# Six recurrent layers on one core: another warm-up for TensorE, the first loads in two blocks each, one subtraction moved on GpSimd, and the two waits of a gather exchanged

## The chip, the core and the metric

The kernel runs on one core of one Trainium2 chip. TensorE (PE) multiplies and transposes into PSUM, VectorE (DVE), ScalarE (ACT) and GpSimd (POOL) do elementwise work, and DMA transfers are issued from the queues of SyncE (SP), ACT and POOL. Each engine runs its own list of instructions in order and meets the others through semaphores. The metric is the device time of one execution in microseconds (us).

## The reference

```python
for i in range(6):                       # n_layers
    gate = ih[i][token]                  # ih: 6 x 4000 x 256, token: 1024
    state = jnp.tanh(state + jnp.matmul(state, hh[i]) * gate)   # state: 1024 x 256, hh: 6 x 256 x 256
return state
```

Everything is float32.

## The kernel before, in words

**Layout.** The state is held transposed: 256 features in two blocks of 128 partitions (c = 0, 1), 1024 tokens along the free dimension. A token's six gate rows lie side by side in DRAM, so one indirect DMA (a gather, L249) brings all six layers' gates for 128 tokens. There are eight gathers, t = 0 to 7, issued one after the other by POOL.

**Tokens equal to the last row of the table** are not fetched. That row is loaded once (L297), spread over all partitions by 12 transposes on PE (L588, three pieces of four), and copied into the gate buffers before the gathers 2 to 7 land over it: DVE does the pieces of layers 0 and 1 (L396), ACT the other two pieces (L302). Gather t waits for the copies to its own tile (the function `gather`, L243 to L253). For tiles 0 and 1 the row is patched in afterwards (L404).

**Layer 0** goes in quarters of 256 tokens (q = 0 to 3). For each, PE multiplies in plain float32 (`plain`, L493, eight products of 128 by 256), DVE multiplies by the gates (`gating`, L420), PE turns the result (`turn`, L502), DVE adds the old state (`sum_up`, L425), and ACT takes the tanh twice: rounded to fp32r into `sh` (L310) and in full into `s` (L314). The low part `sl = s - sh` is a subtraction on POOL (L259), for quarter 0 on DVE (L429).

**Layers 1 to 5** are wide: four units per layer, u = (h, c), half h of the tokens (512) by block c of the features. The weights are split in the same way, a high part on ACT (`round_weights`, L306) and a low part on POOL (`low_weights`, L270). A unit's product is three pairs of products of 128 by 512: high by high (L552), low of weights (L559), low of state (L569). The last pair needs the `sl` of its half of the tokens. DVE multiplies by the turned gates (L436) and adds the state (L441), ACT takes two tanhs (L328, L329), POOL makes `sl` (L265). The gates are turned by PE (`turn_gates`, L521) and copied from PSUM by ACT (L322).

**The order around the change** is written out by hand. PE before layer 0: 5 transposes of the identity matrix as a warm-up (L583), which wait for POOL's identity matrix, then the 12 spread transposes, which wait for the last row, then `plain(0)`, `plain(1)`, `turn(0)`, `plain(2)`, `turn_gates(1, 0, 0)`, `turn(1)`. The weights of layer 2 are loaded from SP once gather 5 has landed. ACT rounds them ahead of the tanh of quarter 2, and POOL takes `low_state(1)`, `low_state(2)`, `low_weights(2)`, `low_state(3)` after the last gather. The first use of `sl` of quarters 2 and 3 is `low_product(1, 1, 0)` on PE.

Of the kernel before, what the change touches and what calls it, by code (L numbers as in the profile page):

```python
# [4 lines left out]
P = 128  # L5
# [16 lines left out]
WIDE = 1  # L22
STEPS = WIDE * QUARTERS
UNITS = HALVES * KC
WARM_UP = 5

# [29 lines left out]
def recurrent_cells(nc, state_t, token, gate_rows, hh, out_t):  # L58
# [10 lines left out]
    with ExitStack() as ctx:  # L69
# [3 lines left out]
        def sem(name):  # L73
            return ctx.enter_context(nc.semaphore(name))
# [44 lines left out]
        spread_ready = sem("spread_ready")  # L119
        state_in = quarter_sems("state_in")  # L120
        w_in = [sem(f"w_in{l}") for l in range(LAYERS)]
        gate_in = [sem(f"gate_in{t}") for t in range(TILES)]
        ident_zero = sem("ident_zero")
        ident_ready = sem("ident_ready")
# [42 lines left out]
        def of_quarter(x, q):  # L167
            return x[:, :, q * QB:(q + 1) * QB]
# [22 lines left out]
        with nc.Block() as block:  # L191

            @block.sync
            def _(sp):
                def load_state(q):
                    sp.dma_start(of_quarter(s, q), state_v[q]).then_inc(state_in[q], 16)

                def load_weights(l):
                    sp.dma_start(w[:, l], w_v[l]).then_inc(w_in[l], 16)

                sp.dma_start(tok[:, :], token).then_inc(tok_in, 16)

                sp.wait_ge(ident_ready, 1)
                load_weights(0)
                sp.wait_ge(tok_in, 16)
                load_state(1)
                sp.wait_ge(state_in[1], 16)
                load_state(2)
                sp.wait_ge(gate_in[1], 16)
                load_state(3)  # L210
                sp.wait_ge(gate_in[2], 16)
                load_weights(1)

                for l, t in LOAD_BEHIND.items():
                    sp.wait_ge(gate_in[t], 16)
                    load_weights(l)
                for l in range(4, LAYERS):
                    sp.wait_ge(w_in[l - 2], 16)
                    load_weights(l)

                def store(u, columns):
                    h, c = divmod(u, KC)
                    sp.dma_start(out_v[h, c, :, columns], of_unit(s, h, c)[:, columns]).then_inc(out_done, 16)

                for u in [0, 1]:
                    sp.wait_ge(unit_s[u], wide_done(LAYERS - 1))
                    store(u, slice(0, HB))
                sp.wait_ge(unit_s[UNITS - 2], wide_done(LAYERS - 1))
                store(UNITS - 2, slice(0, QB))
                sp.wait_ge(unit_s[UNITS - 1], wide_done(LAYERS - 1))  # L230
                store(UNITS - 1, slice(0, QB))
                sp.wait_ge(late_s, 1)
                store(UNITS - 2, slice(QB, HB))

                sp.wait_ge(out_done, 16 * (UNITS + 2))

            @block.gpsimd
            def _(pool):
# [5 lines left out]

                def gather(t):
                    if t not in EARLY_TILES:
                        pool.wait_ge(filled_dve, fills_of(t, DVE_FILLS))
                        pool.wait_ge(filled_act, fills_of(t, ACT_FILLS))
                    nc.gpsimd.indirect_dma_start(  # L249
                        gate[:, t], None, table,  # L250
                        bass.IndirectOffsetOnAxis(row_of[:, t:t + 1].bitcast(u32), 0),
                        bounds_check=last_fetched, oob_is_err=False,
                    ).then_inc(gate_in[t], 16)  # L253
# [20 lines left out]
                    gather(t)  # L274
                low_weights(1)
                low_state(1)
                low_state(2)
                low_weights(2)
                low_state(3)
                for l in range(WIDE, LAYERS - 1):  # L280
                    for h in range(HALVES):
# [13 lines left out]
            @block.scalar  # L295
            def _(act):
                act.dma_start(last_row[:, :, :], last_row_v).then_inc(row_in, 16)  # L297
                act.dma_start(of_quarter(s, 0), state_v[0]).then_inc(state_in[0], 16)

                def fill(i, t, count):  # L300
                    act.wait_ge(spread_ready, i + 1)
# [35 lines left out]
                round_weights(1)  # L337
                tanh(1)
                copy_gates(1, 0, 1)
                round_weights(2)  # L340
                tanh_rounded(2)
                tanh(2)
                copy_gates(1, 1, 0)
                tanh_rounded(3)
# [138 lines left out]
            def _(pe):  # L483
                def plain(n):
                    l, q = divmod(n, QUARTERS)
                    pe.wait_ge(w_in[l], 16)
                    if l == 0:
                        pe.wait_ge(state_in[q], 16)
                    else:
                        pe.wait_ge(s_ready[q], l)  # L490
                    for t in range(TPQ):
                        for c in range(KC):
                            last = nc.tensor.matmul(prod[q][:, t, :], of_quarter(s, q)[:, c, t * P:(t + 1) * P], w[:, l, c, :],  # L493
                                                    start=c == 0, stop=c == KC - 1)
                    last.then_inc(prod_ready[q], 1)
# [78 lines left out]
                def end_product(i, ready):  # L574
# [3 lines left out]
                    low_of_weights(l, h, c, end_bank[i], tokens)  # L578
                    low_of_state(l, h, c, end_bank[i], tokens, ready)

                pe.wait_ge(ident_ready, 1)
                for _ in range(WARM_UP):
                    nc.tensor.transpose(turned[0][:, 0, 0:P], ident[:, :], ident[:, :])  # L583
                pe.wait_ge(row_in, 16)
                for i in range(PIECES):
                    columns = spread[i].rearrange("p (m c) -> p c m", m=P)
# [84 lines left out]
```

## Time and profile before

| | us |
|---|---|
| median of three runs | 59.0 |
| the runs | 58.88, 59.0, 60.3 |
| the profiled execution's own time | 59.24 |
| its span, first to last instruction | 57.4 |
| mean granted TensorE clock | 1.000 |

All times of the rows are microseconds from the span's start. The profiled execution's time is 1.84 us more than its span; that part lies around the instructions and is in no row. "Busy" of an engine is the sum of its instructions; the ends of products are modelled, so two neighbours can overlap in the rows by a few tenths.

### The profile page before, as it was taken

The numbers are of one execution on the slowest core, as the hardware profiler recorded it, in microseconds if no ns is written. First come the engines' busy times: TensorE is split into PE (matmuls) and PEld (weight loads), VectorE is DVE, ScalarE is ACT, GpSimd is POOL, SyncE is SP. The second block draws the span as 40 slices with busy tenths as digits, with TensorE's granted clock in tenths as the row PEclk, the third lists the DMA queues.
The fourth block names the chain that finished last, engine by engine and source line by source line (L and its number), as shares of the span: only waits on it lengthen the run. The fifth ranks groups of instructions, "written<-read, shape, count | busy, mean of one in ns | idle before, by whom it ended". The sixth has DMA issues, their size and how long they took to land.

```text
span 57.4 us, 864 instructions
## 1 busy us (share of the span) xinstructions
PE 50.7 (88%) x271; PEld 42.4 (74%) x271; DVE 39.9 (70%) x62; ACT 43.8 (76%) x80; POOL 41.7 (73%) x40
## 2 busy tenths in 40 slices
PE   0899999989999999699999999999999999999000
PEld 0796888949898796488888988679888798889000
DVE  1249996985995498099985949899089990768700
ACT  0714999565944999968998599999999899943810
POOL 2067176777496299992999995899998998659600
PEclk9999999999999999999999999999999999999999
DMA  0479356574463924000000000000000000004392
GB/s 0 14 242 319 89 181 170 165 220 109 71 198 40 318 49 169 0 0 0 0 0 0 0 0 6 0 6 0 0 0 0 11 0 0 0 0 183 126 323 100
DMA packets 5284, 4.46 MB, mean 78 GB/s; under 512 B 1834, under 2 KB 4906, under 8 KB 5280
## 3 DMA queue, kind: packets, MB, share of 16 engines
q1 hardware_dynamic: 3312, 3.28, 18.0%
q0 software_dynamic: 1152, 0.73, 5.5%
q10 hardware_dynamic: 816, 0.40, 3.0%
q8 instruction: 2, 0.03, 0.2%
q14 instruction: 2, 0.02, 0.1%
HBM read 8.92 MB, written 1.05 MB: 174 GB/s over the span
## 4 chain that ended last, share of the span: by engine, by line
PE 47%; DMA 14%; issue 12%; POOL 11%; ACT 5%; DVE 2%; POOLq 1%; SPq 1%
PE prod L569 14%; PE prod L552 11%; PE prod L559 11%; PE turned L521 11%; DMA gate<-gates_dram,row_of 6%; DMA w<-hh_dram 6%; POOL sl L259 4%; DMA tok<-token_dram 3%; POOL pre L289 2%; POOL wr L270 2%; POOL gate L249 2%; POOLq L191 1%; DVE gp L470 1%; ACT wr L306 1%; ACT sh L310 1%
## 5 line engine op out<-in xcount | busy, mean ns | idle before, releaser
L265 POOL TENSOR_TENSOR sl<-s,sh 128x512 fp32r<-128x512 f32 x16 | 20.4, 1299 | 2.6 <-ACT s L329 2.5
L436 DVE TENSOR_TENSOR prod<-prod,gate_t 128x512 f32<-128x512 f32 x17 | 11.8, 697 | 6.9 <-PE prod L569 6.9
L569 PE MATMUL prod<-sl,wr 128*128 128x512 f32 (+1 forms) x42 | 12.5, 387 | 0.5 <-POOL sl L259 0.5
L552 PE MATMUL prod<-sh,wr 128*128 128x512 f32 (+1 forms) x42 | 12.9, 393 | 0.0
L329 ACT ACTIVATE s<-pre 128x512 f32<-128x512 f32 x18 | 11.3, 630 | 1.7 <-POOL pre L289 1.4
L559 PE MATMUL prod<-sh,wr 128*128 128x512 f32 (+1 forms) x42 | 12.4, 381 | 0.0
L441 DVE TENSOR_TENSOR pre<-prod,s 128x512 f32<-128x512 f32 x17 | 11.8, 692 | 0.6
L249 POOL DMA_INDIRECT gate<-gates_dram,row_of x8 | 8.1, 1007 | 5.1 <-DVE row_of L390 1.8
L328 ACT ACTIVATE sh<-pre 128x512 fp32r<-128x512 f32 x16 | 10.3, 641 | 1.9 <-DVE pre L441 1.9
L322 ACT COPY gate_t<-turned 128x512 f32<-128x512 f32 x20 | 10.8, 585 | 0.0
L521 PEld LDWEIGHTS turned<-ident,gate 128*128 128x128 f32 x80 | 9.1, 140 | 1.5 <-issue 0.8
L521 PE MATMUL turned<-ident,gate 128*128 128x128 f32 x80 | 10.1, 273 | 0.0
L569 PEld LDWEIGHTS prod<-sl,wr 128*128 128x128 f32 x42 | 7.6, 188 | 2.7 <-issue 0.9
L559 PEld LDWEIGHTS prod<-sh,wr 128*128 128x128 f32 x42 | 7.8, 188 | 1.6
L552 PEld LDWEIGHTS prod<-sh,wr 128*128 128x128 f32 x42 | 7.4, 189 | 1.1
L493 PE MATMUL prod<-w,s 128*128 128x256 f32 x32 | 8.0, 400 | 0.1
L270 POOL TENSOR_TENSOR wr<-w,wr 128x512 fp32r<-128x512 f32 x5 | 6.5, 1297 | 1.2 <-issue 0.9
L302 ACT COPY gate<-turned 128x512 f32<-128x512 f32 (+1 forms) x8 | 5.8, 829 | 2.0 <-PE turned L588 1.7
L493 PEld LDWEIGHTS prod<-w,s 128*128 128x128 f32 x32 | 6.2, 203 | 1.3 <-DMA w<-hh_dram 0.5
L259 POOL TENSOR_TENSOR sl<-s,sh 128x512 fp32r<-128x512 f32 x3 | 3.9, 1294 | 1.6 <-ACT s L314 1.6
L404 DVE COPY_PREDICATED gate<-is_last,turned 128x512 f32<-128x512 int32 (+1 forms) x4 | 4.0, 1024 | 0.5 <-ACT gate L302 0.5
L306 ACT CAST wr<-w 128x512 fp32r<-128x512 f32 x5 | 3.2, 632 | 1.5 <-DMA w<-hh_dram 1.5
(35 smaller groups left out, 36.8 us busy)
## 6 DMA issues: line engine op xcount, KB each, us to landing
w<-hh_dram SPq DMA_DIRECT2D x6, 256.0 KB, 2.8
s<-state_t_dram SPq DMA_DIRECT2D x3, 256.0 KB
out_t_dram<-s SPq DMA_DIRECT2D x2, 256.0 KB, 2.1
out_t_dram<-s SPq DMA_DIRECT2D x3, 128.0 KB, 2.0
s<-state_t_dram ACTq DMA_DIRECT2D x1, 256.0 KB, 3.5
gate<-gates_dram,row_of POOLq DMA_INDIRECT x8, 3.3
out_t_dram<-s ACTq DMA_DIRECT2D x1, 128.0 KB, 2.3
tok<-token_dram SPq DMA_DIRECT2D x1, 4.0 KB, 1.7
```

The source lines that it names most:

```text
L249: nc.gpsimd.indirect_dma_start(gate[:, t], None, table, bass.IndirectOffsetOnAxis(row_of[:, t:t + 1].bitcast(u32), 0), bounds_check=last_f ...
L265: nc.gpsimd.tensor_tensor(of_unit(sl[:, l % 2], h, c), of_unit(s, h, c), of_unit(sh[:, l % 2], h, c).bitcast(f32), ALU.subtract).then_inc( ...
L322: nc.scalar.copy(gate_t[:, l % 2, u], turned_bank[u][:, :]).then_inc(gates_copied[u], 1)
L328: nc.scalar.activation(of_unit(sh[:, l % 2], h, c), of_unit(pre, h, c), ACT.Tanh).then_inc(unit_sh[u], 1)
L329: nc.scalar.activation(of_unit(s, h, c), of_unit(pre, h, c), ACT.Tanh).then_inc(unit_s[u], 1)
L436: nc.vector.tensor_tensor(prod_bank[u][:, :], prod_bank[u][:, :], gate_t[:, l % 2, u], ALU.mult).then_inc(unit_gated[u], 1)
L441: nc.vector.tensor_tensor(of_unit(pre, h, c), prod_bank[u][:, :], of_unit(s, h, c), ALU.add).then_inc(unit_pre[u], 1)
L493: last = nc.tensor.matmul(prod[q][:, t, :], of_quarter(s, q)[:, c, t * P:(t + 1) * P], w[:, l, c, :], start=c == 0, stop=c == KC - 1)
L521: last = nc.tensor.transpose(turned_bank[u][:, t * P:(t + 1) * P], gate[:, h * TPH + t, column:column + P], ident[:, :])
L552: nc.tensor.matmul(bank, wr[:, l, k, 0, c * P:(c + 1) * P], of_unit(sh[:, (l - 1) % 2], h, k)[:, tokens], start=k == 0, stop=False, skip_g ...
L559: nc.tensor.matmul(bank, wr[:, l, k, 1, c * P:(c + 1) * P], of_unit(sh[:, (l - 1) % 2], h, k)[:, tokens], start=False, stop=False, skip_gr ...
L569: last = nc.tensor.matmul(bank, wr[:, l, k, 0, c * P:(c + 1) * P], of_unit(sl[:, (l - 1) % 2], h, k)[:, tokens], start=False, stop=k == KC ...
```

## The change

Four edits. PE's warm-up is four products of a constant of ones instead of five transposes of the identity matrix; it waits for no semaphore, and the wait for the identity matrix stands behind it. The state of quarter 0 and the weights of layer 0 are each loaded by two DMAs, one per block c, with a semaphore each; `plain(0)` waits for a block ahead of its first product that reads it. POOL's two waits of a gather are exchanged, with the one on ACT's copies now written first. `low_weights(2)` on POOL goes ahead of `low_state(2)`, and on ACT the rounded tanh of quarter 2 goes ahead of `round_weights(2)`.

```diff
--- before.py
+++ after.py
@@ -22,7 +22,7 @@
 WIDE = 1
 STEPS = WIDE * QUARTERS
 UNITS = HALVES * KC
-WARM_UP = 5
+WARM_UP = 4
 
 
 
@@ -119,6 +119,9 @@
         spread_ready = sem("spread_ready")
         state_in = quarter_sems("state_in")
         w_in = [sem(f"w_in{l}") for l in range(LAYERS)]
+
+        first_state_in = [sem(f"first_state_in{c}") for c in range(KC)]
+        first_w_in = [sem(f"first_w_in{c}") for c in range(KC)]
         gate_in = [sem(f"gate_in{t}") for t in range(TILES)]
         ident_zero = sem("ident_zero")
         ident_ready = sem("ident_ready")
@@ -200,8 +203,10 @@
 
                 sp.dma_start(tok[:, :], token).then_inc(tok_in, 16)
 
+
                 sp.wait_ge(ident_ready, 1)
-                load_weights(0)
+                for c in range(KC):
+                    sp.dma_start(w[:, 0, c], w_v[0][:, c]).then_inc(first_w_in[c], 16)
                 sp.wait_ge(tok_in, 16)
                 load_state(1)
                 sp.wait_ge(state_in[1], 16)
@@ -244,8 +249,8 @@
 
                 def gather(t):
                     if t not in EARLY_TILES:
+                        pool.wait_ge(filled_act, fills_of(t, ACT_FILLS))
                         pool.wait_ge(filled_dve, fills_of(t, DVE_FILLS))
-                        pool.wait_ge(filled_act, fills_of(t, ACT_FILLS))
                     nc.gpsimd.indirect_dma_start(
                         gate[:, t], None, table,
                         bass.IndirectOffsetOnAxis(row_of[:, t:t + 1].bitcast(u32), 0),
@@ -274,8 +279,8 @@
                     gather(t)
                 low_weights(1)
                 low_state(1)
+                low_weights(2)
                 low_state(2)
-                low_weights(2)
                 low_state(3)
                 for l in range(WIDE, LAYERS - 1):
                     for h in range(HALVES):
@@ -295,7 +300,8 @@
             @block.scalar
             def _(act):
                 act.dma_start(last_row[:, :, :], last_row_v).then_inc(row_in, 16)
-                act.dma_start(of_quarter(s, 0), state_v[0]).then_inc(state_in[0], 16)
+                for c in range(KC):
+                    act.dma_start(of_quarter(s, 0)[:, c], state_v[0][:, c]).then_inc(first_state_in[c], 16)
 
                 def fill(i, t, count):
                     act.wait_ge(spread_ready, i + 1)
@@ -337,8 +343,8 @@
                 round_weights(1)
                 tanh(1)
                 copy_gates(1, 0, 1)
+                tanh_rounded(2)
                 round_weights(2)
-                tanh_rounded(2)
                 tanh(2)
                 copy_gates(1, 1, 0)
                 tanh_rounded(3)
@@ -483,13 +489,16 @@
             def _(pe):
                 def plain(n):
                     l, q = divmod(n, QUARTERS)
-                    pe.wait_ge(w_in[l], 16)
-                    if l == 0:
+                    if l > 0:
+                        pe.wait_ge(w_in[l], 16)
+                        pe.wait_ge(s_ready[q], l)
+                    elif q > 0:
                         pe.wait_ge(state_in[q], 16)
-                    else:
-                        pe.wait_ge(s_ready[q], l)
                     for t in range(TPQ):
                         for c in range(KC):
+                            if n == 0 and t == 0:
+                                pe.wait_ge(first_state_in[c], 16)
+                                pe.wait_ge(first_w_in[c], 16)
                             last = nc.tensor.matmul(prod[q][:, t, :], of_quarter(s, q)[:, c, t * P:(t + 1) * P], w[:, l, c, :],
                                                     start=c == 0, stop=c == KC - 1)
                     last.then_inc(prod_ready[q], 1)
@@ -578,9 +587,10 @@
                     low_of_weights(l, h, c, end_bank[i], tokens)
                     low_of_state(l, h, c, end_bank[i], tokens, ready)
 
+                ones = nc.const_aps.tensor(1.0, [P, P], f32)
+                for _ in range(WARM_UP):
+                    nc.tensor.matmul(turned[0][:, 0, 0:P], ones, ones, start=True, stop=True)
                 pe.wait_ge(ident_ready, 1)
-                for _ in range(WARM_UP):
-                    nc.tensor.transpose(turned[0][:, 0, 0:P], ident[:, :], ident[:, :])
                 pe.wait_ge(row_in, 16)
                 for i in range(PIECES):
                     columns = spread[i].rearrange("p (m c) -> p c m", m=P)
```

The list of POOL from its first gather to the first wide low state. L249 and L254 are the gathers, L270 and L275 the low weights of layers 1 and 2, L259 and L264 the low states of quarters 1, 2 and 3. Before:

```order
L249 DMA gate<-gates_dram,row_of 128x1536
L249 DMA gate<-gates_dram,row_of 128x1536 [waits filled_act,filled_dve] x6
L270 TENSOR_TENSOR wr<-w,wr 128x2x256 [waits wh_ready]
L259 TENSOR_TENSOR sl<-s,sh 128x2x256 [waits s_ready1]
L259 TENSOR_TENSOR sl<-s,sh 128x2x256 [waits s_ready2]
L270 TENSOR_TENSOR wr<-w,wr 128x2x256 [waits wh_ready]
L259 TENSOR_TENSOR sl<-s,sh 128x2x256 [waits s_ready3]
```

Now:

```order
L254 DMA gate<-gates_dram,row_of 128x1536
L254 DMA gate<-gates_dram,row_of 128x1536 [waits filled_dve,filled_act] x6
L275 TENSOR_TENSOR wr<-w,wr 128x2x256 [waits wh_ready]
L264 TENSOR_TENSOR sl<-s,sh 128x2x256 [waits s_ready1]
L275 TENSOR_TENSOR wr<-w,wr 128x2x256 [waits wh_ready]
L264 TENSOR_TENSOR sl<-s,sh 128x2x256 [waits s_ready2]
L264 TENSOR_TENSOR sl<-s,sh 128x2x256 [waits s_ready3]
```

The second subtraction for weights moved ahead of the low state of quarter 2, and the two waits of the gathers stand in the other order.

The list of ACT at the same place in the program. L306 and L312 are `round_weights`, L310 and L316 the rounded tanh, L314 and L320 the full tanh, L322 and L328 the copies of turned gates. Before:

```order
L322 COPY gate_t<-turned 128x512 [waits gates_turned1]
L306 CAST wr<-w 128x2x256 [waits w_in2]
L310 ACTIVATE sh<-pre 128x2x256 [waits pre_ready2]
L314 ACTIVATE s<-pre 128x2x256 [waits pre_ready2]
L322 COPY gate_t<-turned 128x512 [waits gates_turned2]
```

Now:

```order
L328 COPY gate_t<-turned 128x512 [waits gates_turned1]
L316 ACTIVATE sh<-pre 128x2x256 [waits pre_ready2]
L312 CAST wr<-w 128x2x256 [waits w_in2]
L320 ACTIVATE s<-pre 128x2x256 [waits pre_ready2]
L328 COPY gate_t<-turned 128x512 [waits gates_turned2]
```

The rounding of layer 2's weights stands between the two tanhs of quarter 2 instead of ahead of both.

## Rows read from the trace of the kernel before

**Rows 1.** By stretch: its length, busy us of PE PEld DVE ACT POOL, granted clock, DMA.

```profile
2.90:5.70 2.80, 2.71 (x13) 2.31 (x12) 2.06 (x5) 0.81 (x3) 2.08 (x2) 1.00 0.86 286
...
30.00:50.00 20.00, 20.00 (x113) 16.91 (x113) 14.48 (x22) 18.83 (x37) 18.17 (x15) 1.00 0.01 2
```

**Rows 2.** The chain that ended last, in order of time: start, us, what.

```profile
2.86 0.18 DVE row_of L390
...
14.67 3.26 DMA w<-hh_dram
...
21.00 1.25 POOL wr L270
22.24 1.26 POOL sl L259
...
23.64 1.16 PE prod L569 x4
...
26.14 0.46 PE prod L559 x2
...
31.14 1.75 PE turned L521 x16
```

**Rows 3.** PE from 20.9 to 27.6: start, us, engine, line, operation, tiles, form, count.

```profile
22.49 0.61 PE L559 MATMUL prod<-sh,wr 128*128 128x512 f32 x2
...
26.43 0.62 PE L569 MATMUL prod<-sl,wr 128*128 128x512 f32 x2
```

**Rows 4.** ACT from 17 to 24.5.

```profile
20.63 0.61 ACT L314 ACTIVATE s<-pre 128x512 f32<-128x512 f32 x1
...
23.70 0.62 ACT L329 ACTIVATE s<-pre 128x512 f32<-128x512 f32 x1
```

**Rows 5.** POOL from 16 to 27; in brackets the idle time ahead and its releaser.

```profile
19.70 1.30 POOL L259 TENSOR_TENSOR sl<-s,sh 128x512 fp32r<-128x512 f32 x1 [1.62 <-ACT s L314]
...
23.44 2.54 POOL L265 TENSOR_TENSOR sl<-s,sh 128x512 fp32r<-128x512 f32 x2
```

**Rows 6.** PE from 9.4 to 13.5.

```profile
9.75 0.60 PE L502 MATMUL turned<-ident,gp 128*128 128x128 f32 x4
...
12.12 0.63 PE L521 MATMUL turned<-ident,gate 128*128 128x128 f32 x4
12.93 0.63 PE L502 MATMUL turned<-ident,gp 128*128 128x128 f32 x4 [0.18 <-DVE gp L420]
```

**Rows 7.** DVE from 7.3 to 13.

```profile
8.91 0.69 DVE L420 TENSOR_TENSOR gp<-prod,gate 128x512 f32<-128x512 f32 x1
10.09 1.31 DVE L404 COPY_PREDICATED gate<-is_last,turned 128x1024 f32<-128x1024 int32 x1 [0.49 <-ACT gate L302]
11.30 0.67 DVE L425 TENSOR_TENSOR pre<-turned,s 128x512 f32<-128x512 f32 x1
12.09 0.69 DVE L420 TENSOR_TENSOR gp<-prod,gate 128x512 f32<-128x512 f32 x1
```

**Rows 8.** POOL's gathers 0, 2 and 5 of the stretch 3 to 14.

```profile
3.31 1.14 POOL L249 DMA_INDIRECT gate<-gates_dram,row_of  x1 [1.79 <-DVE row_of L390]
...
7.02 0.99 POOL L249 DMA_INDIRECT gate<-gates_dram,row_of  x1 [1.28 <-ACT gate L302]
...
11.11 0.99 POOL L249 DMA_INDIRECT gate<-gates_dram,row_of  x1 [0.30 <-issue]
```

**Rows 9.** ACT's second copy of the last row, in the stretch 5.6 to 6.0.

```profile
5.65 0.59 ACT L302 COPY gate<-turned 128x512 f32<-128x512 f32 x1 [0.27 <-issue]
```

**Rows 10.** PE from 0 to 9.8, its first three groups.

```profile
1.58 1.33 PE L583 MATMUL turned<-ident 128*128 128x128 f32 x5 [1.58 <-POOL ident L242]
2.79 2.82 PE L588 MATMUL turned<-ident,last_row 128*128 128x128 f32 x12
5.70 4.21 PE L493 MATMUL prod<-w,s 128*128 128x256 f32 x16
```

**Rows 11.** DVE from 13 to 17.5.

```profile
16.63 0.69 DVE L425 TENSOR_TENSOR pre<-turned,s 128x512 f32<-128x512 f32 x1
```

## The prediction, on record before the changed kernel ran

> **What bounds the kernel now.** I read the stretches first. From 30 to 50 us PE is busy for 20.00 of 20.00 us, ACT for 18.83 and POOL for 18.17 [rows 1]: PE sets the pace of the wide layers, with two engines close behind it, so an edit pays only if it brings PE to that steady stretch earlier. The chain of waits in order of time shows where the steady stretch begins. It runs over the load of layer 2's weights, which lands at 14.67 + 3.26 = 17.93, over the tanhs on ACT to three POOL operations, at 19.70 [rows 5], 21.00 and 22.24, and from their end to PE at 23.64 [rows 2]. PE stands still ahead of 23.64: its last pair before starts at 22.49, and a pair of these products takes 0.46 us from start to next start, so it could have gone on at 22.95. That is a stall of 0.69 us [rows 2, 3].
>
> Then I followed PE back from 22.95. It works without a gap worth naming down to 12.93, where it waited 0.18 us for DVE [rows 6]. Ahead of that DVE is the late one: it starts the multiplication of quarter 1 at 12.09, although its addition for quarter 0 started at 11.30 with 0.67 us in its row; a neighbour can start 0.10 before a row's end, as the 11.30 does after 10.09 + 1.31 = 11.40 [rows 7]. Ahead of 9.75 neither PE nor DVE has slack: PE's turn of quarter 0 starts at 9.75, and DVE's multiplication for it ends at 8.91 + 0.69 = 9.60 [rows 6, 7].
>
> **Edit 1, `low_weights(2)` ahead of `low_state(2)`, with ACT's exchange.** Before, POOL sat idle 1.62 us until the tanh of quarter 2 and then did three operations of 1.25 each in a row [rows 5, 2]. The last of them, the low state of quarter 3, began at 22.24 although its tanh was ready at 20.63 + 0.61 = 21.24 [rows 4]. Now the low weights fill the idle time. DVE's sum for quarter 2 is ready at 16.63 + 0.69 = 17.32 [rows 11], so ACT can take its rounded tanh before the load lands at 17.93, so the rounding of the weights starts at about the same 17.95 and ends near 18.57; the full tanh of quarter 2 ends near 19.1 instead of 19.62. On POOL the low weights then take 18.6 to 19.85, the low state of quarter 2 to 21.1, and the low state of quarter 3 starts at about 21.3 and ends at 22.55. PE, 0.14 us behind the end as before (23.64 - 22.24 - 1.26), could go at 22.69, so PE itself, at 22.95, is the later. The stall of 0.69 is gone. What becomes late next is PE. ACT issues nothing more; its two instructions only change places.
>
> **Edit 2, the gather's waits exchanged.** Gather 2 was issued at 7.02, while ACT's second copy, which it needs, ended at 5.65 + 0.59 = 6.24: 0.78 us between [rows 8, 9]. Gather 0 has one wait only and was issued at 3.31, 0.27 behind DVE's end at 2.86 + 0.18 [rows 8, 2]. I read this as the price of the late wait standing on an instruction of its own, ahead of the gather's preparation. If the exchange puts the late wait on the gather itself, gathers 2 to 7 come 0.5 us earlier at the most (later ones follow at 0.30 behind the one before, [rows 8]); if not, 0. I take 0.5. Its worth is less. DVE's multiplication of quarter 1 waited for gather 3; without that it starts at 11.30 + 0.67 - 0.10, near 11.90, instead of 12.09, as its own queue then ends last: the patch at 10.09, which waits for ACT's copies, and the sum behind it do not move [rows 7]. So PE's turn of quarter 1 comes 0.19 earlier, at 12.74, which is still behind the gate turns that start at 12.12 [rows 6]. Gather 5 at 11.11 moves 0.5 too, and with it the load of layer 2's weights from 14.67 to 14.2, which lands at 17.4 and makes room for edit 1 [rows 2, 8]. **Gain 0.19**, between 0 and 0.25.
>
> **Edit 3, the first loads in blocks.** Each of the two loads needs one more issue. On ACT it lies ahead of a first copy that waits for PE, on SP ahead of a load that waits for the token transfer. A load of 256 KB takes 3.26 us from issue to landing [rows 2]. No row has halves of it. The second block of the weights may land up to 0.4 later (one more issue) or a little earlier than the whole did. `plain(0)` can begin its first product at 5.4, when the spread transposes are through, instead of 5.70, and the other 15 follow from about 5.9 [rows 10]. That makes PE ready for the turn of quarter 0 up to 0.4 earlier, but the turn waits for DVE, which is done at 9.60. I cost it at nothing: what hides it is DVE's path over gathers 0 and 1, whose issues nothing moves. If the cover is gone it is worth 0.4 or costs 0.4.
>
> [...]
>
> **Edit 4, the warm-up.** [...] The 16 products of 256 columns from 5.70 take 4.21, where full pace would give 16 x 0.22 = 3.5 and a tail of 0.1 to 0.2 for the last: some three of them ran at half pace, each costing 0.21. Before the rise PE had worked from 1.58 on, almost without a gap. Now four products run from about 0.75 to 1.6, and PE then stands still until the last row lands at 2.79, 1.2 us that were 0.1 before. Whether the pace rises earlier or later the rows do not tell; at the same moment, the edit is worth nothing, because the spread transposes start at 2.79 either way. I take nothing. From below: all 16 at half pace; from above: the 12 spread transposes faster.
>
> **The sum.** 0.69 + 0.19 = 0.88. One check behind it: PE's low-state pair of layer 2 at 26.43 would start at 25.55 and its second product at 25.78, while POOL's second `sl` of layer 1, ready at 23.44 + 2.54 = 25.98, follows ACT's tanh at 23.70, which moves by 0.19 only [rows 3, 4, 5]. So up to 0.05 is lost there; gain 0.84. The profiled execution's 59.24 becomes 58.40. It lay 0.24 above the median of 59.0, so the median to expect is **58.15**.
>
> **Rivals.**
> *The gain is halved* (chance 0.17). ACT, busy for 94% of the steady stretch, or POOL, for 91% [rows 1], takes the place of the stall, or the exchange moves no gather and the weights' load stays at 17.93. For it: 23.70 moves less than PE. Against it: both have 6 to 9% to catch up with. Half of 0.84 gives 58.6. That the exchange does nothing at all costs 0.19 and lies in the forecast's own range.
>
> *The pace rises earlier* (0.18). Then the spread transposes end up to 1.2 earlier, ACT's copies start up to 0.5 earlier (its table load and the landing of the last row hold the first), and the patch at 10.09 and the sum at 11.30, which hang on them, come 0.5 earlier, in front of gather 3, which with edit 2 is there at 11.2 to 11.5. That adds 0.4 to 0.6: 57.6. [...]
>
> *The pace rises later, slower than before* (0.08). The mechanism is PE's idle 1.2 us behind the ones, with its place in `plain(0)` and `plain(1)`. Three slow products are there now and about three more are hidden by the start at 5.4; each beyond costs 0.21. If all 16 are slow they end at 5.6 + 16 x 0.43 = 12.5 instead of 9.75; with the turn, `plain(2)` and the gate turns behind, the turn of quarter 1 comes at about 15.0 instead of 12.93, 2.1 later, and less the 0.69 that the POOL edit saves this is 1.4: 60.4. It decides from the point where nearly all 16 are slow; a rise in between gives 58.2 to 60 and stands within 2% (0.12).
>
> **The numbers.** The forecast has 0.45, its own range 57.9 to 58.5. A measurement of this kernel tells about 2% from no change: 57.8 and 60.2. Faster by over 2%: the earlier rise, 0.18, and 0.12 of the forecast's lower edge, 0.30. Slower: 0.10, with 0.02 for what no case has. Within 2%: 0.60. The range of 8 in 10 goes from 57.4, which takes in most of the earlier rise, to 59.4, which takes in the halved gain and half of the in-between.
>
> **What the changed profile would show.** Right: no idle time ahead of the first low-state product of units (1, 1), which starts near 22.8; POOL's low weights of layer 2 near 18.5, its last quarter's low state ending by 22.6; gather 2 near 6.5; the turn of quarter 1 near 12.7; the span near 56.5. Wrong: a wait for POOL or ACT in layer 2 that was not there, gather 2 still 0.78 behind ACT's copy, or products of layer 0 at 0.43 spacing past 7.5.

## The result, and the profile after

| | before | changed |
|---|---|---|
| median, 20 executions each | 59.05 us | 58.55 us |
| lowest to highest | 58.57 to 60.3 | 58.3 to 59.33 |
| ratio | | 0.9924 (95%: 0.9899 to 0.9949) |

In a later series the changed kernel had a median of 58.47 against 59.14, ratio 0.9906 (0.9877 to 0.9935). Here and in all experiments the medians are over all executions, and the ratios leave out those more than 1.5% above the fastest of their kernel, among them the changed kernel's 59.33 and, in the experiments, single executions of 104.7 (edit 2 alone) and 62.08 (edits 1 and 2). The kernel is faster, by less than 1% but clear of the uncertainty: by 0.45 and 0.55 us by the ratios and by 0.50 and 0.67 by the medians. The forecast was 0.84 us and 58.15; its direction held, its size did not. The time stands inside the range of 57.4 to 59.4, next to the 58.6 of the rival "the gain is halved".

The first profile of the changed kernel is of its slowest execution, 59.33 us, so a second profile of the same kernel (58.37 us) is read beside it. Rows are as before: start, us, engine, line, operation, tiles, form, count, and in brackets idle time and releaser. First PE's start in the slowest execution:

```profile
0.78 2.05 PE L592 MATMUL turned<-const-float32-1.0 128*128 128x128 f32 x8 [0.78 <-PEq L675]
3.59 2.79 PE L598 MATMUL turned<-ident,last_row 128*128 128x128 f32 x12 [0.76 <-DMA last_row<-gates_dram]
6.17 5.09 PE L502 MATMUL prod<-w,s 128*128 128x256 f32 x16
11.10 0.60 PE L511 MATMUL turned<-ident,gp 128*128 128x128 f32 x4
...
13.70 0.49 PE L511 MATMUL turned<-ident,gp 128*128 128x128 f32 x3
```

and in the other one:

```profile
0.78 2.04 PE L592 MATMUL turned<-const-float32-1.0 128*128 128x128 f32 x8 [0.78 <-PEq L675]
2.85 2.38 PE L598 MATMUL turned<-ident,last_row 128*128 128x128 f32 x12
5.06 3.86 PE L502 MATMUL prod<-w,s 128*128 128x256 f32 x16
10.00 0.66 PE L511 MATMUL turned<-ident,gp 128*128 128x128 f32 x4 [1.08 <-DVE gp L426]
...
12.71 0.63 PE L511 MATMUL turned<-ident,gp 128*128 128x128 f32 x4
```

These answer to [rows 6, 10]. In the good execution PE has a second of slack, 1.08 us, ahead of the turn of quarter 0: nothing that makes its products earlier can help. In the bad one the last row landed at 3.45 (its transfer took 2.70 us, 2.0 in the good one and before), the 16 products took 5.09, and PE itself became the bound, 0.99 us later at the turn of quarter 1. The granted clock reads 1.00 over both halves of that stretch (next rows, the slowest execution; engines as in [rows 1]), so only the pace tells the halves apart: one pass of 256 columns lasted 0.63 us in the first half and 0.38 in the second, 7 passes against 11. Their starts lie 0.43 us apart from 6.17 to 9.16, and behind that 0.22 (9.16, 9.38).

```profile
6.40:9.00 2.60, 2.60 (x7) 2.06 (x7) 2.60 (x4) 2.58 (x5) 1.43 (x2) 1.00 0.50 135
9.00:11.20 2.20, 2.20 (x11) 1.83 (x11) 1.54 (x3) 2.20 (x3) 1.54 (x2) 1.00 0.66 199
```

The place of the stall, in the good execution, answers to [rows 2 to 5]. PE, ACT, POOL:

```profile
22.27 0.62 PE L568 MATMUL prod<-sh,wr 128*128 128x512 f32 x2
22.73 1.09 PE L578 MATMUL prod<-sl,wr 128*128 128x512 f32 x4
...
25.46 0.77 PE L578 MATMUL prod<-sl,wr 128*128 128x512 f32 x2
26.07 0.62 PE L561 MATMUL prod<-sh,wr 128*128 128x512 f32 x2
```

```profile
17.13 0.63 ACT L316 ACTIVATE sh<-pre 128x512 fp32r<-128x512 f32 x1 [0.90 <-DVE pre L431]
17.67 0.60 ACT L312 CAST wr<-w 128x512 fp32r<-128x512 f32 x1
18.18 0.62 ACT L320 ACTIVATE s<-pre 128x512 f32<-128x512 f32 x1
...
23.48 0.62 ACT L335 ACTIVATE s<-pre 128x512 f32<-128x512 f32 x1
```

```profile
18.35 1.29 POOL L275 TENSOR_TENSOR wr<-w,wr 128x512 fp32r<-128x512 f32 x1 [0.48 <-ACT wr L312]
19.60 1.29 POOL L264 TENSOR_TENSOR sl<-s,sh 128x512 fp32r<-128x512 f32 x1
21.09 1.30 POOL L264 TENSOR_TENSOR sl<-s,sh 128x512 fp32r<-128x512 f32 x1 [0.20 <-ACT s L320]
23.14 2.54 POOL L270 TENSOR_TENSOR sl<-s,sh 128x512 fp32r<-128x512 f32 x2 [0.75 <-ACT s L335]
```

The low-state products start 0.46 behind the last high pair, at 22.73: no stall. POOL's last low state is done at 22.39, PE is the later, as forecast (21.09 + 1.30 = 22.39). The gain is not kept whole: the pair at 25.46 lasts 0.77 where such pairs take 0.62, and the next starts 0.61 behind it instead of 0.46.

### The profile page after: what moved, and what is told of

It reads as the page before. It is cut to its first block, busy times and chain, and to the rows that moved or that the text cites. A ratio compares the mean times of both kernels' runs of the same rounds, so it can differ in the third digit from the quotient of the medians.

```text
span 57.5 us, 871 instructions
## 1 busy us (share of the span) xinstructions
PE 51.8 (90%) x274; PEld 44.1 (77%) x274; DVE 39.8 (69%) x62; ACT 43.8 (76%) x80; POOL 41.8 (73%) x40
## 3 DMA queue, kind: packets, MB, share of 16 engines
q1 hardware_dynamic: 3328, 3.28, 17.5%
HBM read 8.92 MB, written 1.05 MB: 173 GB/s over the span
## 4 chain that ended last, share of the span: by engine, by line
PE 82%; DMA 5%; ACT 2%; POOL 2%; POOLq 1%; DVE 1%; issue 1%
PE turned L530 15%; PE prod L578 15%; PE prod L502 15%; PE prod L568 14%; PE prod L561 14%; PE turned L598 5%; DMA last_row<-gates_dram 5%; PE turned L511 3%; POOL pre L294 2%; POOLq L194 1%; DVE gp L476 1%; ACT s L377 1%; ACT s L381 1%; ACT s L379 1%; ACT s L383 1%
## 5 line engine op out<-in xcount | busy, mean ns | idle before, releaser
L270 POOL TENSOR_TENSOR sl<-s,sh 128x512 fp32r<-128x512 f32 x16 | 20.4, 1295 | 2.8 <-ACT s L335 2.6
L254 POOL DMA_INDIRECT gate<-gates_dram,row_of x8 | 8.1, 1007 | 5.4 <-DVE gate L402 1.8
L334 ACT ACTIVATE sh<-pre 128x512 fp32r<-128x512 f32 x16 | 10.2, 640 | 1.4 <-DVE pre L447 1.2
L328 ACT COPY gate_t<-turned 128x512 f32<-128x512 f32 x20 | 10.8, 586 | 0.0
L502 PE MATMUL prod<-w,s 128*128 128x256 f32 x32 | 8.9, 434 | 0.0
L275 POOL TENSOR_TENSOR wr<-w,wr 128x512 fp32r<-128x512 f32 x5 | 6.5, 1296 | 2.2 <-ACT wr L312 2.2
L502 PEld LDWEIGHTS prod<-w,s 128*128 128x128 f32 x32 | 7.0, 227 | 1.1
L316 ACT ACTIVATE sh<-pre 128x512 fp32r<-128x512 f32 x4 | 2.5, 633 | 3.2 <-DVE pre L431 3.2
L402 DVE COPY gate<-turned 128x512 f32<-128x512 f32 (+1 forms) x4 | 3.6, 950 | 1.5 <-PE turned L598 1.5
L431 DVE TENSOR_TENSOR pre<-turned,s 128x512 f32<-128x512 f32 x4 | 2.8, 688 | 2.4 <-PE turned L511 2.4
```

The lines of the kernel that those rows point to most:

```text
L254: nc.gpsimd.indirect_dma_start(gate[:, t], None, table, bass.IndirectOffsetOnAxis(row_of[:, t:t + 1].bitcast(u32), 0), bounds_check=last_f ...
L270: nc.gpsimd.tensor_tensor(of_unit(sl[:, l % 2], h, c), of_unit(s, h, c), of_unit(sh[:, l % 2], h, c).bitcast(f32), ALU.subtract).then_inc( ...
L328: nc.scalar.copy(gate_t[:, l % 2, u], turned_bank[u][:, :]).then_inc(gates_copied[u], 1)
L334: nc.scalar.activation(of_unit(sh[:, l % 2], h, c), of_unit(pre, h, c), ACT.Tanh).then_inc(unit_sh[u], 1)
```

## The experiments

Each kernel was timed against the kernel before in five rounds. The base is the kernel before unless said otherwise.

**Edit 1 alone.** On POOL and on ACT:

```diff
                 low_state(1)
+                low_weights(2)
                 low_state(2)
-                low_weights(2)
...
-                round_weights(2)
                 tanh_rounded(2)
+                round_weights(2)
```

> The kernel before with edit 1 alone (low weights of layer 2 ahead of the low state of quarter 2, with the exchange on ACT). Theory A (the stall of 0.69 us ahead of the low-state products is won in full, and the rest of the forecast was lost in the start of the program): the stall is gone and the median is 0.5 to 0.7 us below the kernel before, ratio 0.988 to 0.992. Rival B (the stall is only partly a loss, because ACT and POOL take its place): 0.1 to 0.4 us, ratio 0.993 to 0.998.

Measured: median 58.69 against 59.15, ratio 0.9927 (0.9891 to 0.9964). The stall is gone in its profile, PE:

```profile
22.59 0.62 PE L559 MATMUL prod<-sh,wr 128*128 128x512 f32 x2
23.05 1.09 PE L569 MATMUL prod<-sl,wr 128*128 128x512 f32 x4
```

This edit alone gives 0.43 us (0.21 to 0.64) of the whole, between the two expectations: the stall is gone, as theory A says, and a part comes back as a wait of PE in layer 2, as rival B says; the pair there takes 0.78.

**Edit 2 alone.**

```diff
+                        pool.wait_ge(filled_act, fills_of(t, ACT_FILLS))
                         pool.wait_ge(filled_dve, fills_of(t, DVE_FILLS))
-                        pool.wait_ge(filled_act, fills_of(t, ACT_FILLS))
```

> The kernel before with edit 2 alone (the two waits of a gather exchanged). In the changed kernel's profile gather 2 followed ACT's copy by 0.27 us, 0.78 before. The forecast's term says: DVE's multiplication of quarter 1 no longer waits for gather 3, the turn of quarter 1 comes 0.2 us earlier and so does everything behind it, ratio 0.996 to 0.998. Rival: POOL's stall ahead of the low-state products grows by the same 0.2 us, because its low state of quarter 2 still hangs on the load of layer 2's weights, and nothing is won: ratio 0.999 to 1.001, a stall of 0.7 to 0.9 us ahead of those products.

Measured: 58.82 against 59.14, ratio 0.9949 (0.9916 to 0.9981). The profile does what the rival says: PE is ready at 22.34 + 0.46 = 22.80, 0.15 us earlier than before, and the stall is as much longer, 0.83, since the load of the weights lands when it did. PE:

```profile
22.34 0.61 PE L559 MATMUL prod<-sh,wr 128*128 128x512 f32 x2
23.63 0.70 PE L569 MATMUL prod<-sl,wr 128*128 128x512 f32 x2 [0.68 <-POOL sl L259]
```

Gather 5 was issued at 10.42, 0.69 earlier than before, but landed no earlier: the weights' load behind it was issued at 14.88, 14.67 before [rows 2, 8], and ACT's rounding began at 17.95 as before. The timing says 0.1 to 0.5 us faster, which takes in the forecast's 0.19; the one profile gives no gain. Its execution, at 59.23, lies 0.41 above the median of its own kernel, so it need not be typical, but no other was profiled, and why the two differ is not shown. ACT:

```profile
17.95 0.62 ACT L306 CAST wr<-w 128x512 fp32r<-128x512 f32 x1 [1.68 <-DMA w<-hh_dram]
```

**Edits 1 and 2.**

> The kernel before with edits 1 and 2, its start untouched. If the two terms of the forecast add up: 0.69 + 0.19 less what layer 2 takes back, 0.7 to 0.85 us faster than before, ratio 0.986 to 0.988. If only edit 1 counts: the same as edit 1 alone, 0.43 us, ratio 0.991 to 0.994. What layer 2 takes back should show as one wait of PE for POOL's low state of 0.1 to 0.2 us, as it did after edit 1 alone.

Measured: 58.52 against 59.14, ratio 0.9895 (0.9858 to 0.9931), 0.62 us. The turn of quarter 1 starts at 12.78, 13.03 after edit 1 alone, and the low-state products at 22.79 against 23.05: in these two profiles edit 2 moves the program by 0.25 once edit 1 has freed POOL. The ratios of the two kernels, 0.9895 and 0.9927, lie 0.19 us apart, which their uncertainty covers. What layer 2 takes back is there too, in the last row. PE:

```profile
12.78 0.63 PE L502 MATMUL turned<-ident,gp 128*128 128x128 f32 x4
...
22.79 1.09 PE L569 MATMUL prod<-sl,wr 128*128 128x512 f32 x4
...
25.52 0.79 PE L569 MATMUL prod<-sl,wr 128*128 128x512 f32 x2
```

**Edit 3 alone.** Two loads per block, as in the diff of the change.

```diff
-                load_weights(0)
+                for c in range(KC):
+                    sp.dma_start(w[:, 0, c], w_v[0][:, c]).then_inc(first_w_in[c], 16)
```

> The kernel before with edit 3 alone (first loads in two blocks each). In the changed kernel's profile the last row landed 2.70 us behind its issue, 2.0 before. Rival C (the added issues delay that landing): the landing is near 2.7 us again and the median is 0.2 to 0.8 us above the kernel before. Theory A (the landing varies by itself): landing 2.0 to 2.7 with no link to the blocks, median within 0.15 us of before.

Measured: 59.1 against 59.15, ratio 1.000 (0.9957 to 1.0042). PE started its spread transposes at 2.71, so the last row was not late: rival C, that the blocks delay it, is out. The stall was 0.41 here (23.32 less 22.91), because the load of layer 2's weights happened to land at 17.63, 0.3 earlier than in [rows 2]. PE:

```profile
22.45 0.61 PE L563 MATMUL prod<-sh,wr 128*128 128x512 f32 x2
23.32 0.94 PE L573 MATMUL prod<-sl,wr 128*128 128x512 f32 x3 [0.26 <-POOL sl L262]
```

ACT's rounding behind the load's landing:

```profile
17.63 0.62 ACT L310 CAST wr<-w 128x512 fp32r<-128x512 f32 x1 [1.22 <-DMA w<-hh_dram]
```

**Edit 4 alone.**

```diff
+                ones = nc.const_aps.tensor(1.0, [P, P], f32)
+                for _ in range(WARM_UP):
+                    nc.tensor.matmul(turned[0][:, 0, 0:P], ones, ones, start=True, stop=True)
                 pe.wait_ge(ident_ready, 1)
-                for _ in range(WARM_UP):
-                    nc.tensor.transpose(turned[0][:, 0, 0:P], ident[:, :], ident[:, :])
```

> The kernel before with edit 4 alone (eight passes of ones from 0.8 us on instead of five transposes from 1.6 on). Theory A: no work is saved, the medians differ by less than 0.15 us. Rival D (the earlier work brings the full pace forward): 0.2 to 0.5 us faster. Rival E (it puts it off): 0.2 to 0.8 us slower.

Measured: 59.1 against 59.15, ratio 1.0006 (0.9975 to 1.0038). Neither D nor E. With ones from 0.78 on, the 16 products of layer 0 took 4.24 in this kernel's slowest execution, the profiled one, and 4.21 with the transposes [rows 10]. Over all profiles the time of these products varies more between executions than between the two warm-ups: 3.72 to 5.09 in five with the ones, 3.72 to 4.21 in eight with the transposes. PE:

```profile
0.78 2.05 PE L583 MATMUL turned<-const-float32-1.0 128*128 128x128 f32 x8 [0.78 <-PEq L666]
2.96 2.79 PE L589 MATMUL turned<-ident,last_row 128*128 128x128 f32 x12
5.64 4.24 PE L493 MATMUL prod<-w,s 128*128 128x256 f32 x16
```

**The changed kernel without edit 3** (edits 1, 2 and 4).

> The changed kernel without edit 3: the first loads in one transfer each, as before. Rival C (blocks delay the last row): 0.3 to 0.8 us faster than the changed kernel, near 57.9, last row landing near 2.0 us. Theory A: the same as the changed kernel within 0.15 us, 58.4 to 58.7.

Measured: 58.51 against 59.15, ratio 0.9886 (0.9849 to 0.9922), within theory A. Its profile also answers the prediction's rival of the earlier rise. The full pace came while the spread transposes still ran: the 12 took 2.17 us and were through at 4.99, 0.62 earlier than before. That bought nothing behind them, since DVE waited for the gate rows of quarter 1, and PE's turn of quarter 1 came at 12.78, as in the profile of edits 1 and 2. PE, then DVE:

```profile
2.82 2.17 PE L589 MATMUL turned<-ident,last_row 128*128 128x128 f32 x12
```

```profile
11.94 0.69 DVE L420 TENSOR_TENSOR gp<-prod,gate 128x512 f32<-128x512 f32 x1 [0.27 <-DMA gate<-gates_dram,row_of]
```

**The changed kernel without edit 4** (edits 1, 2 and 3).

> The changed kernel without edit 4: five transposes behind the identity matrix as the warm-up. Theory A (start edits are worth nothing in the median): within 0.15 us of edits 1 and 2 alone and of the changed kernel. Rival D (the ones bring the full pace forward in some executions): slower than the changed kernel by 0.1 to 0.3 us in the median, with more executions 0.5 us or more above the fastest.

Measured: 58.48 against 59.14, ratio 0.9913 (0.9881 to 0.9945). Theory A; rival D's slower median and wider spread (58.37 to 58.8) did not come.

**The changed kernel again.**

> The changed kernel again, on the chip of the three before it. Measured first: ratio 0.9924. Theory A: 0.990 to 0.994 again, within 0.15 us of edits 1 and 2 alone; the profile's last row lands nearer 2.0 us behind its issue than 2.7. Rival C (the blocks delay the last row): slower than edits 1 and 2 alone by 0.2 us or more, landing 2.7 again.

Measured: 58.47 against 59.14, ratio 0.9906 (0.9877 to 0.9935), as theory A says. Its profile is the good execution above, with the last row landed 2.0 us behind its issue.

**The changed kernel with ACT's rounding of layer 3 behind the first wide tanhs.**

```diff
                 copy_gates(1, 1, 1)
-                round_weights(3)
                 wide_tanh(1, 0, 0)
                 wide_tanh(1, 0, 1)
+                round_weights(3)
```

> The changed kernel with ACT's rounding of layer 3's weights moved from ahead of layer 1's first wide tanhs to behind the first two pairs. In five profiles with edit 1 PE lost 0.1 to 0.2 us in its first low-state pair of layer 2, waiting for POOL, whose low state waited for ACT. Theory F (this is what took back part of the stall's 0.69, and ACT's queue is its cause): the pair takes 0.62 again instead of 0.78, and the kernel is 0.1 to 0.2 us faster than the changed one, ratio to before 0.987 to 0.990. Rival G (POOL's own 1.25 us per operation is the cause): no difference.

Measured: 58.52 against 59.12, ratio 0.9896 (0.9852 to 0.9941), six executions. In the profile theory F holds. ACT's tanhs of layer 1 start at 21.50, 21.91 in the changed kernel, so one rounding earlier, POOL's low states at 22.73, 23.14 in the changed kernel, and the pair on PE takes 0.61. POOL, then PE:

```profile
22.73 2.56 POOL L270 TENSOR_TENSOR sl<-s,sh 128x512 fp32r<-128x512 f32 x2 [0.22 <-ACT s L335]
```

```profile
25.55 0.61 PE L578 MATMUL prod<-sl,wr 128*128 128x512 f32 x2
26.00 0.62 PE L561 MATMUL prod<-sh,wr 128*128 128x512 f32 x2
```

The next pair starts 0.45 behind it, 0.61 in the changed kernel: 0.16 us. The timing cannot tell that from the changed kernel's 0.9906 to 0.9924.

**Edits 1 and 2 with the same move.**

> Edits 1 and 2 with the same move on ACT, the start as before the change. Theory F: 0.1 to 0.2 us faster than edits 1 and 2 alone, ratio 0.986 to 0.989. If the edits at the start were worth something after all, this one stays behind the changed kernel with the move by that amount; theory A says within 0.15 us.

Measured: 58.38 against 59.12, ratio 0.989 (0.9851 to 0.993), the lowest median of all, with six executions. It is not behind the changed kernel with the move, so the timing shows no worth of the edits at the start here either.

**The load of layer 2's weights one gather earlier,** no other edit.

```diff
-LOAD_BEHIND = {2: 5, 3: 7}
+LOAD_BEHIND = {2: 4, 3: 7}
```

> The kernel before, with the load of layer 2's weights issued behind gather 4 instead of gather 5, and no other edit. Theory H (the stall of PE was the late landing of that load, which held ACT's tanh and through it three POOL operations in a row): the rounding no longer waits, the stall falls from 0.69 to 0.2 or less, ratio 0.990 to 0.994, as edit 1 alone. Rival I (POOL's order makes the stall whatever the load does): the stall stays above 0.5 and the ratio is 0.998 to 1.001.

Measured: 58.78 against 59.12, ratio 0.9955 (0.9923 to 0.9987). The load landed at 17.03 and the stall is gone (23.08, 0.47 behind the pair at 22.61), with POOL's order as before: theory H, the late load made the stall. But only 0.27 us came of it, less than theory H gave. PE waits in layer 2 here too (the pair there takes 0.80), and there is a new wait ahead: the load is now issued at 13.7, while gather 5 is still in transfer, that gather lands at 10.76 + 4.38 = 15.14, DVE waits for it, and the turn of quarter 2 on PE comes 3.53 us behind that of quarter 1, 3.07 before (the rows of before have the first of the two, 12.93 [rows 6]; the other stood at 16.00). PE at the former stall, DVE's wait, and PE's two turns:

```profile
22.61 0.62 PE L559 MATMUL prod<-sh,wr 128*128 128x512 f32 x2
23.08 1.09 PE L569 MATMUL prod<-sl,wr 128*128 128x512 f32 x4
```

```profile
15.27 0.69 DVE L420 TENSOR_TENSOR gp<-prod,gate 128x512 f32<-128x512 f32 x1 [0.74 <-DMA gate<-gates_dram,row_of]
```

```profile
12.57 0.63 PE L502 MATMUL turned<-ident,gp 128*128 128x128 f32 x4 [0.16 <-DVE gp L420]
...
16.10 0.41 PE L502 MATMUL turned<-ident,gp 128*128 128x128 f32 x2 [0.31 <-DVE gp L420]
```

**The changed kernel without a warm-up.**

```diff
-WARM_UP = 4
+WARM_UP = 0
```

> The changed kernel without any warm-up. It prices what the prediction left at nothing. Theory A (a late rise of the pace costs 0.21 us for each product of layer 0 beyond those hidden by DVE's path): the first products stay at a spacing of 0.43 us until 7 to 9 us, up to six of them more than hidden, the kernel 0.1 to 0.9 us slower than the changed one and the executions spread by more. Rival J (DVE's path over gathers 0 and 1 hides it all): the median moves by less than 0.1 us.

Measured: 58.62 against 59.12, ratio 0.9927 (0.9901 to 0.9954). The profiled execution took 58.98 us, the slowest of the eleven and 0.61 above the changed kernel's good one, and its turn of quarter 1 is as much later, 13.32 against 12.71. PE:

```profile
2.89 2.79 PE L598 MATMUL turned<-ident,last_row 128*128 128x128 f32 x12 [2.89 <-DMA last_row<-gates_dram]
5.56 5.32 PE L502 MATMUL prod<-w,s 128*128 128x256 f32 x16
10.72 0.60 PE L511 MATMUL turned<-ident,gp 128*128 128x128 f32 x4
...
13.32 0.60 PE L511 MATMUL turned<-ident,gp 128*128 128x128 f32 x4
```

The products took 5.32 instead of 3.86 and PE was through with them at 10.88 instead of 8.92, 1.96 later; of that, DVE's path hid 1.35. So the price that theory A gives to a late rise is real in this execution. The median lies only 0.07 to 0.15 above the changed kernel's, and the ratios cannot tell the two kernels apart: rival J is not ruled out for most executions.

## Why the prediction was right in kind and wrong in size

**Edit 1, the stall: the mechanism held, and this is the term that failed, 0.69 where 0.43 was measured.** The stall of 0.69 went to nothing in all kernels with the edit, and PE, not POOL, ends last at its place. Two things were mis-sized. First, it was read from one execution and taken in full. The stall depends on when the load of layer 2's weights lands: the profiles with POOL's order and the load as before show 0.69, 0.41 and 0.79 (0.83 with edit 2 alone), where ACT's rounding behind that landing starts at 17.95, 17.63 and 18.30 (17.95). The forecast then also subtracted the 0.24 us by which that execution lay above the median, although a part of these 0.24 can be the stall itself. Second, the allowance behind the sum was 0.05 us for PE's wait in layer 2 and the runs show 0.15 to 0.19 (0.77 to 0.81 against 0.62). That allowance let PE start the moment POOL's `sl` was ready and left out the 0.14 us from POOL's end to PE's start that the prediction itself had read at the stall. The engines moved about as it said: in the good profile ACT's tanh stands at 23.48, 0.22 earlier (0.19 forecast), and POOL is done at 23.14 + 2.54 = 25.68, when PE's second product of the pair, 0.23 behind the 25.46, would be due; what is lost is the handover. Moving one rounding on ACT brings POOL 0.41 us forward there and removes the wait, so ACT's queue set it, and not POOL's own speed. Measured alone the edit gave 0.43 us.

**Edit 2: the number came out, the path only in part.** Gather 2 follows ACT's copy by 0.26 instead of 0.78. In the slowest execution ACT's copy ended at 6.42 + 0.59 = 7.01 and the gather was issued at 7.27. ACT, then POOL:

```profile
6.42 0.59 ACT L308 COPY gate<-turned 128x512 f32<-128x512 f32 x1 [0.27 <-PE turned L598]
```

```profile
7.27 0.98 POOL L254 DMA_INDIRECT gate<-gates_dram,row_of  x1 [1.53 <-DVE gate L402]
```

The turn of quarter 1 came at 12.71 and 12.78 against a forecast of 12.74. But the forecast said that DVE would then wait for no gather. In the profile without edit 3 it still waited 0.27 us for one, at 11.94, though POOL had issued gather 3 at 7.39, 0.92 earlier than before: it took 4.4 us to its landing, and the multiplication started only 0.15 earlier than the 12.09 of before. And the sum ahead of it on DVE, which the forecast held at 11.30, came at 11.05 in the good profile. The side claim that the weights' load would then land 0.5 earlier failed in the profile of edit 2 alone: gather 5 was issued 0.69 earlier, but took 4.44 us to its landing at 10.42 + 4.44 = 14.86, and the load went out at 14.88, 14.67 before. In the good profile of the changed kernel it did come earlier, issued at 14.4 and landed 2.8 us later.

**Edit 3: right.** Worth nothing, with the cover that was named: with the blocks layer 0's products start at 5.06 and without them at 5.53 (the profile without edit 3), and in both PE then waits for DVE, 1.08 and 0.68 us. Alone, with two loads of 128 KB each in place of one of 256 KB for the state of quarter 0 and for the weights of layer 0, the edit cost nothing: ratio 1.000 with an uncertainty of 0.4%.

**Edit 4: nothing, as forecast, but one sentence of the working was wrong.** I counted four products of ones ending at 1.6 us and an idle 1.2 us behind them. The trace shows eight rows for these four calls, in 2.05 us from 0.78 to 2.83 (`e4_ones`, L583), two for each call; the spread transposes follow at 2.82 to 2.96 in the four profiles with the ones where the last row is in time. The same count stood in the rows of before, 16 products for the eight calls of `plain(0)` and `plain(1)` [rows 10], and I didn't carry it over. The two paces it counts with are in the traces: transposes start (2.82 - 1.33)/7 = 0.21 us apart at the beginning [rows 10] and 1.75/16 = 0.11 in the wide layers [rows 2], products of 256 columns 0.43 and 0.22 (the changed kernel's slowest execution). So the idle time of the slower rival was not in the kernel when the last row was in time. In the slowest execution, where the row was late, PE did stand idle for 0.76 us behind the ones, and there the full pace came late; whether the idle time is the cause is not shown, and the transposes of before would have left PE idle too.

**The later pace is real all the same.** In the changed kernel's slowest execution it came with a late last row: 5.09 us of products, 0.99 later at the turn of quarter 1, which ate the whole gain of the stall. That execution lies at 59.33, beside 59.24 for the profiled one of before. The forecast had left this in the bounds of a rival, not in the sum. How many executions pay it is not shown; one profile in the changed kernel's two did. The earlier rise, the rival with the chance of 0.18, came too, in the profile without edit 3 and in the good profile, and the turn of quarter 1 came no earlier for it than in the profile of edits 1 and 2 (12.78, 12.71 and 12.78).

**What is left.** From the profiled 59.24 the forecast was 58.40, and the good profiles are at 58.37 (changed) and 58.48 (edits 1 and 2): against that one execution the sum came out. Partly that is luck. The stall cost a little more than 0.69: from the start of the low-state products to the next group PE took 1.00 us behind the wait (24.64 less 23.64) and 0.92 without it, and these 0.08 made up for most of what layer 2 took back beyond the 0.05 allowed. Before, then the changed kernel:

```profile
24.64 1.03 PE L521 MATMUL turned<-ident,gate 128*128 128x128 f32 x8
```

```profile
23.65 1.04 PE L530 MATMUL turned<-ident,gate 128*128 128x128 f32 x8
```

Against the median the sum did not come out: the ratio gives 0.45 and 0.55, the medians 0.50 and 0.67. The size of the stall in other executions may close most of that gap. Less their stalls, the profile of before and that of edit 3 alone lie together, 59.24 - 0.69 = 58.55 and 58.94 - 0.41 = 58.53. The profile of edit 4 alone comes to 59.59 - 0.79 = 58.80, with its turn of quarter 1 0.24 us later than before (13.17). By that a median execution of before, 59.05 to 59.15, has a stall of 0.5 to 0.6 us. This is an estimate from three profiles, and no profile of a median execution shows it. With the 0.08 added and the 0.16 of layer 2 taken off, edit 1 is then worth 0.4 to 0.5, and 0.43 was measured; with 0.15 to 0.22 for edit 2 the whole is 0.6 to 0.7. What is missing to 0.45 and 0.55 is within the uncertainty of the ratios.

Products of ones instead of transposes as the warm-up made no difference in time, ratio 1.0006. In the profile with the earlier load the pace rose while PE had done nothing but transposes: of the 12 spread transposes, all ahead of the first product, the median lasted 421 ns, and the shortest, at the end of them, 273, as the transposes of the wide layers did (L521 in the profile of before, 270 to 273 ns from 31.0 to 47.3). The view of that line (shortest, median and longest in ns):

```profile
L588 PE MATMUL turned<-ident,last_row x12: 273/421/473, 2.7 to 5.0; 128*128 128x128 f32 x12
```

## What to carry to other kernels

A wait that hangs on a DMA's landing had no one length here, 0.41 to 0.83 us for the stall in four profiles: read such a wait in several executions before it goes into a sum, and forecast against the median of runs rather than the one profile. If only one profile is there, do not take its stall in full and subtract its excess over the median as well. When a stall on the bounding engine is removed, look at once which queue is only a few tenths behind there, since it takes part of the gain back, and count the time from that engine's end to the next one's start; here POOL did, behind one rounding on ACT. Where a gather waits for two semaphores, the order of the two waits was worth half a microsecond of its issue: the wait that ends last is now written first. That it then rides on the gather itself is my reading; the runs show only the 0.26 against 0.78.

## What the runs showed of the hardware that was not expected

The four products of ones, 128 by 128 in float32, show as eight rows of PE, two for each call, in 2.04 to 2.05 us (`e4_ones`, L583, and both profiles of the changed kernel, L592); the five transposes of the identity matrix show as five, in 1.33, and the 12 spread transposes as 12 [rows 10]. The pace of PE rose at very different moments in executions of one kernel. In the changed kernel's good execution it rose during the spread transposes: they took 2.38 us, 2.79 in its slowest, and the shortest lasted 273 ns, 421 there. In the slowest it rose near 9 us: the products of layer 0 start 0.43 us apart up to 9.16, and 0.22 apart behind that. With edit 2 alone, gather 5, issued 0.69 us earlier, did not let the load behind it go earlier (14.88 against 14.67). The landing of one small transfer, the last row's 6 KB, which the program lays out in 384 pieces of 16 bytes, took 1.9 to 2.1 us in thirteen profiles and 2.70 in one, and in that one PE waited 0.76 us for it and started the spread transposes at 3.59, 2.70 to 2.96 in the others. In the profile with the earlier load, where the 256 KB of layer 2's weights were issued at 13.71 before gather 5 had landed, gather 5 took 4.38 us from issue to landing, and DVE then waited 0.74 us for it; that the load is the cause is not shown, since with edit 2 alone the same gather took 4.44 and landed before that load was issued.
